# A macaron block on one core: the first sequence's expert layer computed dense, every step placed anew, two normalisations moved to ScalarE

## The reference, cut to what matters

```python
x: [4, 1024, 128]
x = x + 0.5 * ffn(layernorm(x))
x = x + mixer(layernorm(x))
x = x + 0.5 * ffn(layernorm(x))

# ffn: 8 experts, the best 2 of each token
logits = tokens @ router_w.T
vals, idx = top_k(logits, 2);  weights = softmax(vals)
out_all = gelu(tokens @ w1[e]) @ w2[e]         # w1[e] 128x256, w2[e] 256x128
output = sum over the two chosen e of weights * out_all[e]

# mixer: per sequence of 1024 rows
v = x @ value_W.T
gates = sigmoid(x @ gate_W.T)                  # 9 gates of 128
out = v * gate_0 + sum over 8 shifts s of roll(v, -s) * gate_s
return (out - mean) * rsqrt(var + eps) * gamma + beta
```

## Time and profile before

| what | us |
|---|---|
| median of 3 runs | 508.68 (504.05 to 509.39) |
| the profiled execution's own time | 505.95 |
| its span, first to last instruction | 504.2 |

### The profile page before, as it was taken

The page is one execution under the profiler, slowest core; times in us unless marked ns, Lnnn a source line. Parts: engine busy times, 40 slices in busy tenths (PEclk is TensorE's granted clock), DMA queues, the critical chain, the costliest instruction groups (busy, mean ns, idle before and its releaser), DMA issues.

```text
span 504.2 us, 8967 instructions
## 1 busy us (share of the span) xinstructions
PE 347.4 (69%) x2115; PEld 283.8 (56%) x2115; DVE 286.4 (57%) x1076; ACT 181.6 (36%) x422; POOL 254.5 (50%) x264
## 2 busy tenths in 40 slices
PE   1341885688899889996959977499753986288300
PEld 1330885587567756775537764277643975187300
DVE  6558054006666899889993699954997260020011
ACT  1010542343466456552425533355421342044100
POOL 0177717377767204767056173272664747570172
PEclk9999998798999999997779976889985798589955
DMA  8944447558527633453264242543447445845321
GB/s 253 297 142 137 148 136 225 158 157 254 178 88 203 190 106 89 121 157 115 69 183 121 86 150 90 155 111 101 145 150 215 135 142 166 245 128 155 101 73 47
DMA packets 102176, 74.66 MB, mean 148 GB/s; under 512 B 9704, under 2 KB 98032, under 8 KB 102128
## 3 DMA queue, kind: packets, MB, share of 16 engines
q1 hardware_dynamic: 93936, 57.30, 39.3%
q0 software_dynamic: 8192, 16.79, 11.2%
HBM read 48.50 MB, written 25.56 MB: 147 GB/s over the span
## 4 chain that ended last, share of the span: by engine, by line
PE 54%; DVE 15%; issue 12%; POOL 6%; DMA 5%; ACT 4%; SPq 2%; POOLq 0%; ACTq 0%; DVEq 0%
PE ps_u L341 16%; PE ps_u L402 14%; PE ps_d L353 14%; PE ps_t L331 5%; DMA xg<-xs 3%; PE ps_r L373 3%; DVE x_res L658 3%; POOL xs L759 3%; POOL g L771 3%; DVE prod L677 2%; DVE acc L680 2%; ACT y L476 2%; DVE stats L568 1%; DVE xn L588 1%; PE ps_t L395 1%
## 5 line engine op out<-in xcount | busy, mean ns | idle before, releaser
L771 POOL DMA_INDIRECT g<-ys,slot x128 | 127.2, 994 | 139.8 <-DMA ys<-y 86.1
L759 POOL DMA_INDIRECT xs<-xn,slot x128 | 126.3, 987 | 101.1 <-DVE slot L642 64.2
L341 PE MATMUL ps_u<-xT,w1s 128*128 128x128 f32 x736 | 114.7, 306 | 12.7 <-issue 9.9
L341 PEld LDWEIGHTS ps_u<-xT,w1s 128*128 128x128 f32 x736 | 106.0, 221 | 15.4 <-issue 11.6
L353 PE MATMUL ps_d<-w2s,hT 128*128 x736 | 105.3, 287 | 12.5 <-ACT y L476 11.4
L353 PEld LDWEIGHTS ps_d<-w2s,hT 128*128 128x128 f32 x736 | 95.1, 200 | 21.6 <-issue 21.6
L469 ACT ACTIVATE hT<-ps_u 128x512 f32<-128x512 f32 x96 | 55.6, 579 | 142.4 <-PE ps_d L353 126.8
L331 PE MATMUL ps_t<-ident,xg 128*128 128x128 f32 x184 | 43.5, 322 | 55.5 <-issue 48.8
L658 DVE SCALAR_TENSOR_TENSOR x_res<-g,wk,x_res 128x128 f32<-128x128 f32 x128 | 37.8, 348 | 75.3 <-DMA g<-ys,slot 74.0
L402 PE MATMUL ps_u<-xm,mixT 128*128 128x512 f32 x160 | 78.2, 622 | 0.4 <-ACT xm L453 0.4
L331 PEld LDWEIGHTS ps_t<-ident,xg 128*128 128x128 f32 x184 | 25.1, 162 | 75.2 <-issue 65.3
(11 more groups left out here) (79 smaller groups left out, 218.7 us busy)
## 6 DMA issues: line engine op xcount, KB each, us to landing
w1s<-in_L_ffn_w_dram SPq DMA_DIRECT2D x184, 128.0 KB
ys<-y SPq DMA_DIRECT2D x88, 128.0 KB, 2.1
xg<-xs SPq DMA_DIRECT2D x24, 384.0 KB, 4.4
xs<-zeros SPq DMA_DIRECT2D x10, 256.0 KB, 4.5
xg<-xs SPq DMA_DIRECT2D x8, 320.0 KB, 6.2
x_res<-in_L_attn_x_dram SPq DMA_DIRECT2D x4, 512.0 KB, 5.2
xs<-xn,slot POOLq DMA_INDIRECT x128
g<-ys,slot POOLq DMA_INDIRECT x128
```

The costliest lines, as they stand in the source:

```text
L341: i = pe.matmul(bank[:, c:c + P], w1s[:, G % NW, t, k * P:(k + 1) * P], xT[:, G % 2, t * P:(t + 1) * P], start=True, stop=True)
L759: pool.indirect_dma_start(out=xs[n % 2], out_offset=bass.IndirectOffsetOnAxis(ap=slot[:, n % RING, k, j:j + 1], axis=0), in_=xn[:, n % 2, ...
L771: pool.indirect_dma_start(out=g[:, k, j, :], out_offset=None, in_=ys[n % 2], in_offset=bass.IndirectOffsetOnAxis(ap=slot[:, n % RING, k, j ...
```

## The change

Four parts.

1. Sequence 0's first expert layer is computed **dense**: all eight experts' w1 are loaded once (`w1d`), and for 2 halves of 512 rows times 8 experts (16 steps i) PE does two `up` matmuls of 128x512 and eight `down` matmuls of 128x128 into `ps_d`, ACT two Gelus, and DVE adds the product, weighted by a weight that is zero for experts not chosen (`w_all`), to `x_res` (`dense_add`, four instructions). Segment 0's scatter, load, stores, gather and combine are gone. `down` of step i+1 waits for `dense_add` of step i.
2. The routings of segments 1, 2 and 3, and the mixer weights' transposes, hang on the dense steps. Segment 4 is routed in segment 2 (router at step 5, rank at step 8), 5 in 4 and 6 in 5 (steps 2 and 4, as before), 7 in 6 (steps 3 and 5).
3. Sequence 0's mixer now lies wholly in segment 1 (2 units at step 3, 3 at steps 4 to 9, `turn_mixed` at step 11). The others stay. SP issues segment 5 to 7's row loads at step 9 of the segment before, ahead of that step's w1 load and store, and segment 4's at step 2 of segment 3. DVE's order is written out.
4. Two normalisations go from DVE to ACT, as `Identity` activations with a scale and a bias per partition: `xn2` (`normalise2`, 8 instructions, ahead of the copies of `turn_norm2`) and the mixer's sum (`normalise_mixed`, 8 instructions, at `Z_AT`). DVE only makes the bias, and `out_add` becomes three 128x1024 instructions.

```diff
-    NG = NSEG * PAIRS
+    NG = (NSEG - 1) * PAIRS
+    NDENSE = 2 * E
+    ROUTER_IN = {0: 1, 5: 2, 11: 3}
+    RANK_IN = {1: 1, 7: 2, 13: 3}
+    MIXW_IN = {8: 0, 9: 1, 10: 2}
+    ROUTED = {2: (4, 5, 8), 4: (5, 2, 4), 5: (6, 2, 4), 6: (7, 3, 5)}
+    NORM2_AT = {(1, 3): 0, (2, 10): 1, (3, 10): 2, (4, 10): 3}
+    MIXED_AT = {(1, 11): 0, (3, 8): 1, (4, 8): 2, (5, 8): 3}
+    UNITS_AT = {0: {(1, 3): 2, (1, 4): 3, (1, 5): 3, (1, 6): 3, (1, 7): 3, (1, 8): 3, (1, 9): 3}}
+    for s in range(1, BATCH):
+        UNITS_AT[s] = {(s + 1, 10): 4, (s + 1, 11): 4, **{(s + 2, q): 2 for q in range(6)}}
+    Z_AT = {(2, 0): 0, (3, 11): 1, (4, 11): 2, (5, 10): 3}
+    LOAD_AT = {(2, 1): 3, (3, 2): 4, (4, 9): 5, (5, 9): 6, (6, 9): 7}
+    MOVES = [("to", 1), ("to", 2), ("to", 3), ("from", 1), ("to", 4), ("from", 2)]
+    for n in range(5, NSEG):
         MOVES += [("from", n - 2), ("to", n)]
     MOVES += [("from", NSEG - 2), ("from", NSEG - 1)]
...
         @block.sync
+            load_x(0)
+            sp.dma_start(rt_raw[:], router_w).then_inc(s_rt, 16)
+            load_x(1)
+            sp.dma_start(w1d[:], w1.rearrange("e d f -> d e f")).then_inc(s_w1d, 16)
...
                 for q in range(PAIRS):
+                    if (n, q) in LOAD_AT:
+                        load_rows(LOAD_AT[n, q])
+                    if pair_of(n, q) + NW < NG:
+                        load_w1(pair_of(n, q) + NW)
+                    store_y(pair_of(n, q))
...
         @block.tensor
+            def dense_up(i):
+                half, e = divmod(i, E)
+                for k in range(FH):
+                    bank = product_bank(("dense", i, k))
+                    pe.matmul(bank, w1d[:, e, k * P:(k + 1) * P], xd[:, half, :], start=True, stop=True).then_inc(s_u, 1)
+
+            def dense_down(i):
+                half, e = divmod(i, E)
+                pe.wait_ge(s_uread, product_at["dense", i, FH - 1] + 1)
+                if i:
+                    pe.wait_ge(s_dread, i)
...
+                for j in range(HT):
+                    for k in range(FH):
+                        t = pe.matmul(ps_d[:, j * D:(j + 1) * D], hd[:, i % 2, k, j * P:(j + 1) * P],
+                                      w2s[:, e, k * D:(k + 1) * D], start=(k == 0), stop=(k == FH - 1))
+                t.then_inc(s_dense, 1)
...
+            for i in range(NDENSE):
+                if i + 1 < NDENSE:
+                    dense_up(i + 1)
+                dense_down(i)
+                if i in ROUTER_IN:
+                    turn_norm(ROUTER_IN[i])
+                    router(ROUTER_IN[i])
+                if i in MIXW_IN:
+                    turn_mix_weights(MIXW_IN[i])
+                if i in RANK_IN:
+                    rank(RANK_IN[i])
...
         @block.scalar
+            def normalise2(s):
+                act.wait_ge(s_shift2, s + 1)
...
+                for j in range(TPS):
+                    t = act.activation(xn2[:, j, :], x_res[:, s * TPS + j, :], ACT.Identity, scale=rstd[:, 1, j:j + 1],
+                                       bias=shift[:, 1, j:j + 1])
+                    if j % HT == HT - 1:
+                        t.then_inc(s_xn2, 1)
+
+            def normalise_mixed(s):
+                act.wait_ge(s_shift, s + 1)
...
+                for j in range(TPS):
+                    t = act.activation(z_mix[:, j, :], o_mix[:, j, :], ACT.Identity, scale=rstd[:, 2, j:j + 1],
+                                       bias=shift[:, 0, j:j + 1])
+                t.then_inc(s_z, 1)
...
         @block.vector
+            def dense_add(i):
+                half, e = divmod(i, E)
+                dve.wait_ge(s_dense, i + 1)
...
+                for j in range(HT):
+                    xt = x_res[:, half * HT + j, :]
+                    t = dve.scalar_tensor_tensor(xt, ps_d[:, j * D:(j + 1) * D], w_all[:, 0, e, half * HT + j:half * HT + j + 1],
+                                                 xt, ALU.mult, ALU.add)
+                t.then_inc(s_dread, 1)
...
             def out_add(s):
...
+                dve.wait_ge(s_z, s + 1)
+                link(dve.tensor_tensor(z_mix[:], z_mix[:], gamma_b[:].unsqueeze(1).broadcast_to([P, TPS, D]), ALU.mult))
+                dve.tensor_tensor(x_seq(s), x_seq(s), z_mix[:], ALU.add).then_inc(s_omix, 1)
...
+            norm(0)
+            norm(1)
+            choose(0)
+            weigh(0)
+            weigh_all()
+            for i in range(NDENSE):
+                dense_add(i)
...
+            norm2(0)
+            for u in range(1, U):
+                gate(0, u)
+            out_stats(0)
+            out_add(0)
+            norm(4)
+            choose(4)
+            places(4)
+            combine_all(1)
+            norm2(1)
...
```

More of the change, by code:

```diff
@@ L72, in units_at, with pair_of, place_of, use_of @@
     def units_at(n, q):
[L74 to L79, removed]
-        return 0, range(0)
+        for s, at in UNITS_AT.items():
+            if (n, q) in at:
+                before = sum(c for k, c in at.items() if k < (n, q))
+                return s, range(before, before + at[n, q])
+        return 0, range(0)
+    def pair_of(n, q):
+        return (n - 1) * PAIRS + q
+    def place_of(G):
+        return G // PAIRS + 1, G % PAIRS
+    def use_of(n):
+        return (n - 1) // 2
     def seq_of(n):
@@ L444, in _ @@
                         mix_unit(s, i)
-                    if routed_in(n) is not None and q == rank_step(n):
-                        rank(routed_in(n))
-                down(first + PAIRS - 1)
+                    if n in ROUTED and q == ROUTED[n][2]:
+                        rank(ROUTED[n][0])
+                down(pair_of(n, PAIRS - 1))
         @block.scalar
@@ L550, in _ @@
                         unit(s, i)
-                    if routed_in(n) is not None and q == rank_step(n):
-                        gap_tanh(routed_in(n))
-                copy_y(first + PAIRS - 1)
+                    if n in ROUTED and q == ROUTED[n][2]:
+                        gap_tanh(ROUTED[n][0])
+                    if (n, q) in Z_AT:
+                        normalise_mixed(Z_AT[n, q])
+                copy_y(pair_of(n, PAIRS - 1))
         @block.vector
@@ L745, in _ @@
-            for k in range(GROUPS):
-                combine(NSEG - 1, k)
+            norm(0)
[3 more added lines that the diff above has]
+            weigh_all()
+            for i in range(NDENSE):
+                dense_add(i)
+                if i == 0:
+                    choose(1)
+                if i == 1:
+                    places(1)
+                if i == 3:
+                    norm(2)
+                if i == 6:
+                    choose(2)
+                if i == 8:
+                    places(2)
+                if i == 9:
+                    norm(3)
+                if i == 12:
+                    choose(3)
+                if i == 14:
+                    places(3)
@@ new lines, in _ @@
+            norm2(0)
[8 more added lines that the diff above has]
+            norm2(1)
+            gate(1, 1)
+            gate(1, 2)
+            for u in range(3, U):
+                gate(1, u)
+            combine_all(2)
+            norm2(2)
+            out_stats(1)
+            gate(2, 1)
+            gate(2, 2)
+            out_add(1)
@@ new lines, in _ @@
+            norm(5)
+            gate(2, 3)
+            gate(2, 4)
+            choose(5)
+            gate(2, 5)
+            places(5)
+            for u in range(6, U):
+                gate(2, u)
+            combine_all(3)
+            norm2(3)
+            out_stats(2)
+            gate(3, 1)
+            gate(3, 2)
+            out_add(2)
+            norm(6)
+            gate(3, 3)
+            gate(3, 4)
+            choose(6)
+            gate(3, 5)
+            places(6)
+            for u in range(6, U):
+                gate(3, u)
@@ L748, in _ @@
+            combine_all(4)
+            out_stats(3)
+            out_add(3)
+            norm(7)
+            choose(7)
+            places(7)
+            combine_all(5)
+            combine_all(6)
+            combine_all(7)
         @block.gpsimd
```

310 lines of the change are left out of this document (151 added, 159 removed).

## The result

| | us |
|---|---|
| changed kernel, median of 4 runs | 531.93 (528.2 to 533.43) |
| kernel before, beside it | 507.15 |
| ratio | 1.050, 95% interval 1.044 to 1.056 |
| the profiled execution's span | 526.2 (before 504.2) |

The change costs 5%. The forecast was no change, and the measured time lies outside its range.

The account below looks back on a forecast made before the run. No engine was taken to bound the whole: PE bounds segments 0 to 2, DVE segments 3 and 4. Stages summed to segment 7's start at 435.3, plus a tail of 67.3, span 502.6; forecast 506, range 491 to 520.

Parts of the forecast that it names:

- the dense stage gives back what the empty opening saves: Opening and first segment: 6.4 us longer, segment 1 at 101.5 against 95.1, though 50 us without expert work are gone.
- the two waits of 4.2 and 3.1 us behind the norms: Dense stage: PE waits behind DVE's norm of 6.9 us, 4.2 at step 5 and 3.1 at step 11.
- hole at step 10 of segment 2: Segment 2: PE stands some 9 us while DVE does places, combine and norm2's statistics strictly in order.
- a chain of its own: Segments 5 and 6: stores, gather and scatter make 56.1 us load to load, first transpose 5.1 later, at 435.3.
- third rival: Dense stage: its holes bring a lower clock, some 10 us stay on the path, 516 in all; chance 0.29.
- the stretch of segments 1 to 4: Segments 1 to 4 take 48.9, 58.6, 52.0 and 63.7 us, so segment 5 starts at 324.7.
- ScalarE's sets: Normalisations on ACT: 2.4 us for eight instructions; in segment 3, 1.3 ahead of the copies and 2.4 for `normalise_mixed`.
- second rival: ACT, 36% busy, finds gaps for its normalisations; DVE's saving in segment 4 counts: about 10 us less, 496; chance 0.18.
- the early row loads: Segment ends: segment 4's load wait of 5.7 us is gone, and segment 6's load comes at 374.1, before at 379.58.
- the late rank in segment 5: Segments 5 and 6: rank at 23.8 us, slots 3.2 later, at 351.7.

Follow-up runs that it names:

- e1: The changed kernel with both normalisations back on VectorE, all places kept: 514.67 us, 1.020 of the kernel before.
- e3: The changed kernel with segment 3's row loads at step 9 of segment 2 and segment 4's at step 8 of segment 3: 520.75 us, 1.035.
- e2: e3 with VectorE's combine of segment 1 and second norm of sequence 1 ahead of the places of segment 4: 515.55 us, 1.026.
- e7: The changed kernel with the edits of e1, e3 and e2 together: 507.72 us, 1.007.
- e9: The kernel before with only the mixer's input normalised on ScalarE, VectorE's order kept: 518.2 us, 1.031.
- e16: e7 with two dense-stage norms cut in two, segment 2 gathered before segment 4's scatter, segment 4's rows loaded at step 11 of segment 3: 495.83 us, 0.976.
- e14: The kernel before with row loads of segments 1 to 3 at step 8 and of 4 to 7 at step 10 of the segment before: 487.6 us, 0.965.
- e4: The kernel before with only part 4 of the change, both normalisations on ScalarE: 526.51 us, 1.050.
- e11: e4 with the 64 ScalarE instructions as Copy without scale and bias, so the mixer's two normalisations are left out: 523.42 us.

## Why the prediction was wrong

**What held.** That the dense stage gives back what the empty opening saves: segment 1 started at 103.5, forecast 101.5, before 95.1 (four other executions with the same dense stage, e1, e3, e2 and e7, have 103.8 to 106.0), and the two waits of 4.2 and 3.1 us behind the norms were 3.83 and 3.90. That DVE's order makes a hole at step 10 of segment 2: forecast 9, measured 10.85. From the rank of segment 4 to the bias of `norm2` DVE took 14.0 us, forecast 13.7. That segment 7's start hangs on a chain of its own: from segment 6's load (396.4) to segment 7's first transpose 61.3 us, forecast 61.2. The third rival, a lower clock in the dense stage, fell: the window shows 0.94.

**The step that failed** is the stretch of segments 1 to 4, forecast 3.7 us too short for segment 1, 6.3 for segment 2 and 6.6 for segments 3 and 4 together. Two terms of it are wrong.

The first is a mis-sized term, ScalarE's sets. The sum took 2.4 us for eight instructions from a row without pointer operands; they take 3.19. And where the mixer's input is normalised it counted 1.3 us a set (segment 3 and the second rival), about the half set that stands ahead of the first transposes. At step 10 of segment 2 the trace of e9 shows 3.5: the copies behind the transposes stand behind the whole set, the normalisation that had been ready in advance is now done while PE waits, and PE comes back at the half clock (four transposes in 1.12 us, where eight take 1.04). Part 4 costs 15 to 17 us in the changed kernel and 21 to 25 in the kernel before. The second rival, that the sets find gaps because ACT is 36% busy, is refuted. Its own sum was off, too: 3 x 1.3, 2 x 2.4 and the 4 us of DVE are 12.7, not "about 10".

The second is a term that was missing. The prediction priced the early row loads only at the segment ends, where they help, and not at steps 1 and 2, where 1.5 MB go ahead of a w1 load. The kernel before has such a wait, in segment 0, and it was not carried into the sum:

```profile
82.29 2.05 PE L341 MATMUL ps_u<-xT,w1s 128*128 128x128 f32 x8 [5.00 <-issue]
```

e3 gives 7 to 11 us, with two waits of 5.0 and 2.6 us and the half clock behind both. In segment 2 the wait comes ahead of the rank, and DVE's chain to step 10 starts at the rank, so the hole there can't take it up:

```profile
193.66 0.33 PE L402 MATMUL ps_r<-m_cnt,later 128*128 128x64 f32 x2
```

That is 37.7 us into segment 2, where the forecast had 31.3. In e3's profiled execution segments 2 and 3 took 57.7 and 51.0 us, forecast 58.6 and 52.0: there the missing term is the whole difference. What e3 still has too much lies in segment 1 (52.1, forecast 48.9), segment 4 (68.2, forecast 63.7) and segments 5 and 6 (117.2, forecast 110.6).

The part of the sum that goes with part 4 of the change was about 10 us by the second rival, so 5 to 7 are missing for the sets, and 7 to 11 for the loads: 515 to 521 of the 526, if the two add. That is not shown: e7, with both and e2's edit, gave 24 us where the three had 33 one by one. The rest, the late rank in segment 5 among it (27.6 us after its start, forecast 23.8), was not traced to a cause.

**Why the dense idea shows no gain of its own.** Repaired step by step it goes from 532 to 496 (e16), which beats the kernel before, but the kernel before repaired in the same respect goes to 488 (e14). Both issue their row loads at steps 8 to 11. By the profiled executions (e16's is 4 us above its median) e16 starts segment 1 13.1 us later than e14 (102.7 against 89.6), wins 11.0 in segment 3, which has no routing (51.0 against 62.0), and loses 10.6 in segments 4, 5 and 6 together. That the dense form loses 6 (by the ratios) to 8 us to the other one when both are placed well is a comparison of these two versions; a better order for the dense form was not searched for.

## What to carry to other kernels

An engine that is idle most of the time is no free place for work if its order is fixed and the next copy that the bound engine needs stands behind that work: look where in its order the work would stand, and whether it was finished in advance before. A large load moved to an earlier step goes ahead of every small one behind it on that queue, so ask which of them is due within its transfer time. When a wait is taken away, look at the next queue on the same path (here POOL's) before adding up gains.

## What the runs showed of the hardware

A 128x128 ScalarE instruction from SBUF takes 484 ns with scale and bias from SBUF (Identity, e4) and 300 ns with neither (Copy, e11); eight in a row 3.19 and 1.7 us. A VectorE addition of 128x128 that reads PSUM takes 344 ns on average, no more than the 349 ns that the same operation from SBUF (L768, `combine`) takes in the same trace, and four in a row took 1.13 us (at 50.16 in the changed kernel), so the 1.2 taken from the earlier trace rows was right. Its group in the changed kernel:

```profile
L759 DVE SCALAR_TENSOR_TENSOR x_res<-ps_d,w_all,x_res 128x128 f32<-128x128 f32 x64 | 18.0, 344 | 30.2 <-PE ps_d L456 30.1
```
